# Two-layer conditional block on one core: another order of the first loads, and tile 5 copied ahead in step 0

## The chip, the cores and the metric

The kernel runs on one core of a Trainium2 chip. The metric is the device time of one execution in microseconds (us). The kernel before took 1658.18 us, the median of 3 runs (1657.36 to 1660.54). Its profile comes from one further execution, which took 1657.96 us; the profiled span of the core in it is 1656.2 us.

## What is computed

x is (64, 128, 512): 64 batches of 128 rows. Each batch b has a category (0 to 63) and an expert (0 to 15):

```python
# layer 0: one 512x512 matrix and bias per batch, chosen by category
x = x + (einsum('bsd,bdh->bsh', x, W[cat_ids]) + b[cat_ids][:, None, :])
# layer 1: fc1 to 2048, gelu, 384 shared columns, and 128 columns of the batch's expert
h = gelu(einsum('bnd,hd->bnh', x, fc1_w) + fc1_b, approximate=False)
shared = einsum('bnh,sh->bns', h, fc2_w) + fc2_b
expert = einsum('bnh,bph->bnp', h, experts_w[indices]) + experts_b[indices][:, None, :]
x = x + concatenate([shared, expert], axis=-1)
```

All of it is float32. The kernel makes each float32 product out of three matmuls on `fp32r` operands: each operand is split into a high half (a conversion on ScalarE) and a low half (the whole less the high half, on VectorE), and high x high, high x low and low x high are added up.

## The kernel before

The batches are worked through in 16 groups of four. A group's main work is 16 steps (`body`, c = 0 to 15). In step c TensorE does the fc1 of a block of 128 hidden columns (line 797: twelve matmuls of 512 columns into `ps_e` or `ps_h`), ScalarE its gelu (line 542), VectorE its two halves (`h_high`, line 671, and `h_low`), and TensorE, one step later, fc2 with the shared and the expert columns (line 812: twelve matmuls into `ps_out`). Experts' weights are transposed on VectorE (line 646) and halved. Layer 0 of the next group is spread over the steps of this one.

Nothing of that kind hides layer 0 of group 0: it is a stage of its own ahead of the steps, and the change is about it. It has 16 "slices", four for each of the four batches (`l0_slice`, line 772). A slice is a [128, 512] part of a category's matrix (256 KB), loaded by SyncE (`load_w`, line 340) into one of eight slots (four in `w_raw`, four in `e_blocks`), halved by ScalarE (`w_high`, line 491) and VectorE (`w_low`, line 610), and used in three matmuls (line 784). Slice j may be loaded once slice j - 8 is halved (`w_lo`), and ScalarE halves slice j three slices ahead of TensorE, and not before slice j - 5 is done (`l0_done`). The fourth slice of a batch comes with two matmuls that add the bias row (line 782, from `b0_rows`).

A batch's x is loaded as it is (`load_first_x`), transposed on TensorE (`turn_x`), and halved (`x_high`, `x_low`). When its four slices are done VectorE adds x to the product (`y_sum`, line 632), TensorE transposes the sum (`turn_y`, line 754) and it is halved into `y_t`, which fc1 reads; fc1 of group 0 wants all four batches.

Beside this the weights of fc1 and fc2 are prepared in 28 tiles (`PREP`): each is loaded by ScalarE's queue (`load_prep`, line 306), transposed on TensorE (`turn_prep`, line 761), and halved (`prep_high`, line 531, `prep_low`, line 604). Tiles 0 to 4 are done in the first stage (tile 0 at its start, tiles 1 to 4 ahead of slices 2, 5, 8 and 11), tiles 5 to 27 in the steps of group 0, two in each. From tile 5 on a transpose waits for the low half of the tile before it (`prep_lo`), since all go through the one bank `ps_t`. A tile's load waits until the tile before it in its buffer is transposed, and is issued behind that tile's `prep_high`.

The order of everything is written out by hand, one program for each engine, and each engine takes its instructions in that order; semaphores join them. SyncE's queue before the change issues `cats`, x of batch 0, waits for `cats`, and then goes slice by slice, with the bias row behind the first slice of a batch, the next batch's x behind the third, `exps` and `b1` behind slice 1, a wait for `exps` behind slice 2, and the reads of four expert indices from there (lines 399 to 418). ScalarE's queue issues tiles 0, 1 and 2 at its start. The experts' first quarter follows in SyncE's queue (lines 419 and 420).

Of the kernel before, what the change touches and what calls it, by code (L numbers as in the profile page):

```python
# [26 lines left out]
P = 128  # L27
# [3 lines left out]
def build(nc, x, cat_ids, exp_ids, l0_w, l0_b, fc1_w, fc1_b, fc2_w, fc2_b, exp_w, exp_b, out):  # L31
# [5 lines left out]
    GB = 4  # L37
# [9 lines left out]
    S0SLOTS = 5  # L47
    AHEAD = 3
    L0_STEPS = (2, 3, 5, 7, 9, 10, 11, 12)
    PSLOTS = 3  # L50
    Q = 32
    NPREP = NC + NS * NQ
# [2 lines left out]
    with ctx:  # L55
# [6 lines left out]
        def sem(name):  # L62
            return ctx.enter_context(nc.semaphore(name))
# [49 lines left out]
        cats_in = sem("cats_in")  # L113
        exps_in = sem("exps_in")
        prep_in = [sem(f"prep_in{i}") for i in range(PSLOTS)]
        w0_in = [sem(f"w0_in{i}") for i in range(W0SLOTS)]
        w_in = [sem(f"w_in{i}") for i in range(WSLOTS)]
        y_stored = sem("y_stored")
        y_blocks_in = sem("y_blocks_in")
# [41 lines left out]
        def after(eng, s, value):  # L161

            if not (isinstance(value, int) and value <= 0):
                eng.wait_ge(s, value)

        def first(G):

            return isinstance(G, int) and G == 0
# [102 lines left out]
        def w_slot(G, j):  # L271
            if first(G) and j % W0SLOTS >= WSLOTS + 2:
                return e_blocks[:, 1, j % W0SLOTS - WSLOTS - 2, :]
            return w_raw[:, j % (W0SLOTS if first(G) else WSLOTS), :]
# [39 lines left out]
        def _(sp):  # L314
# [8 lines left out]
            def load_first_x(b):  # L323

                sp.dma_start(resid[:, b, :], x[b, :, :]).then_inc(first_x_in[b], 16)

            def load_x_blocks(G, b):
# [7 lines left out]
                for i in range(P // Q):  # L335
                    src = x[bass.ds(G * GB + b, 1), :, :].rearrange("o (j q) (i n) -> i q (o j) n", q=Q, n=P)[i]
                    sp.dma_start(x_blocks[i * Q:(i + 1) * Q, :].rearrange("q (j n) -> q j n", n=P), src)\
                      .then_inc(x_blocks_in, 16)

            def load_w(G, j, cat):  # L340

                if first(G):
                    after(sp, w_lo, j - W0SLOTS + 1)
                else:
                    after(sp, w_lo, G * NC + j - WSLOTS + 1)
                k = j % KD
                src = l0_w[bass.ds(cat, 1), :, :].rearrange("o (p k) n -> k (o p) n", k=KD)[k]
                sp.dma_start(w_slot(G, j), src)\  # L348
                  .then_inc(w0_in[j % W0SLOTS] if first(G) else w_in[j % WSLOTS], 16)

            def load_b0(G, b, cat):
                after(sp, xb_ready, (G - 1) * GB + b)
# [2 lines left out]
            def category(G, b):  # L355
                return index(cats, G * GB + b, l0_w.shape[0])
# [40 lines left out]
                      .then_inc(out_stored, 16)  # L397

            sp.dma_start(cats[:, :], cat_ids.rearrange("(o n) -> o n", o=1)).then_inc(cats_in, 16)
            load_first_x(0)  # L400
            sp.wait_ge(cats_in, 16)
            first_experts = []
            for j in range(NC):
                if j % KD == 0:
                    cat = category(0, j // KD)
                load_w(0, j, cat)
                if j % KD == 0:
                    sp.dma_start(b0_rows[:, j // KD, :], l0_b[bass.ds(cat, 1), :]).then_inc(b0_rows_in[j // KD], 16)
                if j % KD == KD - 2 and j // KD + 1 < GB:
                    load_first_x(j // KD + 1)  # L410
                if j == 1:
                    sp.dma_start(exps[:, :], exp_ids.rearrange("(o n) -> o n", o=1)).then_inc(exps_in, 16)
                    sp.dma_start(b1[:, :].rearrange("p (u c) -> p u c", c=QUAD), fc1_b.rearrange("(u p c) -> p u c", p=P, c=QUAD))\
                      .then_inc(b1_in, 16)
                if j == 2:
                    sp.wait_ge(exps_in, 16)
                if 2 <= j < 2 + GB:
                    first_experts.append(index(exps, j - 2, exp_w.shape[0]))
            load_experts(0, 0, first_experts, range(GB))
            load_experts(0, 1, first_experts, [0])  # L420

# [67 lines left out]
        @block.scalar  # L489
        def _(act):  # L490
            def w_high(G, j):
                if first(G):
                    act.wait_ge(w0_in[j % W0SLOTS], 16 * (j // W0SLOTS + 1))
                else:
                    after(act, w_in[j % WSLOTS], 16 * ((G - 1) * (NC // WSLOTS) + j // WSLOTS + 1))
                after(act, l0_done, j - S0SLOTS + 1 if first(G) else G * NC + j - 1)
                nc.scalar.copy(split_slot(G, j)[:, 0, :], w_slot(G, j)).then_inc(w_hi, 1)  # L497

            def x_high(G, b):
                after(act, x_turned, G * GB + b + 1)  # L500

                after(act, l0_done, G * NC + (b - 1 if first(G) else b) * KD)
                nc.scalar.copy(x_halves(G, b)[:, 0, :, :], x_whole(G)).then_inc(x_hi, 1)  # L503

            def y_high(G, b):
                after(act, y_turned, G * GB + b + 1)
                after(act, fc1_done, G * NC)
                nc.scalar.copy(y_t[:, 0, :, b, :], y_whole(G, b)).then_inc(y_hi, 1)

            def store_y(G, b):  # L510
                after(act, y_ready, G * GB + b + 1)
                act.dma_start(y_rows[b, :, :], y[:, b, :]).then_inc(y_stored, 16)

            def load_y_blocks(G, b):
                after(act, y_stored, 16 * ((G - 1) * GB + b + 1))
                if b + 1 < GB:
                    after(act, x_turned, G * GB + b + 2)
                else:
                    after(act, y_turned, G * GB + b)
                for i in range(P // Q):  # L520
                    src = y_rows[b, :, :].rearrange("(j q) (i n) -> i q j n", q=Q, n=P)[i]
                    act.dma_start(x_blocks[i * Q:(i + 1) * Q, :].rearrange("q (j n) -> q j n", n=P), src)\
                       .then_inc(y_blocks_in, 16)

            def e_high(g, c):
                after(act, e_turned, g * NC + c + 1)
                after(act, fc2_done, (g * NC + c - 1) * GB)
                nc.scalar.copy(experts_of(c % 2, 0), e_whole[:, :].rearrange("p (q v n) -> p q v n", q=GB // 2, v=2))\  # L528
                    .then_inc(e_hi, 1)

            def prep_high(t):
                if t is None:
                    return
                act.wait_ge(prep_turned, t + 1)
                nc.scalar.copy(prep_dst(t, 0), four(prep_bank(t))).then_inc(prep_hi, 1)
                for u in prep_later(t):
                    load_prep(act, u)

            def gelu(g, c):
                after(act, fc1_done, g * NC + c + 1)  # L540
                after(act, h_lo, g * NC + c - 1)
                nc.scalar.activation(g_raw[:, c % 2, :], h_bank(c)[:, :], ACT.Gelu, bias=b1[:, c:c + 1])\  # L542
                    .then_inc(gelu_done, 1)

            for t in range(PSLOTS):
                load_prep(act, t)

            act.wait_ge(ident_ready, 1)
            nc.scalar.activation(g_raw[:, 0, 0:1], ident[:, 0:1], ACT.Gelu)
            prep_high(0)  # L550
            x_high(0, 0)
            for j in range(AHEAD):
                w_high(0, j)
            for j in range(NC):

                if j + AHEAD < NC:
                    w_high(0, j + AHEAD)
                if j % KD == 1 and j > KD:
                    y_high(0, j // KD - 1)
                if j % KD == KD - 2 and j // KD + 1 < GB:  # L560
                    x_high(0, j // KD + 1)
                for t in prep_beside(j):
                    prep_high(t)
            y_high(0, GB - 1)
            act.wait_ge(b1_in, 16)

            def body(g, more):
                for c in range(NC):

                    if more:  # L570
                        for j in slices_in(c):
                            w_high(g + 1, j)
                        for b in begun_in(c):
                            x_high(g + 1, b)
                    e_high(g, c)
                    if more:
                        for b in summed_in(c - 1):
                            store_y(g + 1, b)
                        for b in summed_in(c - 2):
                            load_y_blocks(g + 1, b)  # L580
                    gelu(g, c)
                    for n in range(PREP_RATE):
                        prep_high(prep_in_step(g, c, n))
                if more:
                    for b in range(GB):
                        y_high(g + 1, b)

            groups(act, body)


        @block.vector
        def _(dve):
# [112 lines left out]
            def body(g, more):  # L705
                for c in range(NC):
# [8 lines left out]
                    if c == 0 and not first(g):  # L715
                        for b in range(GB):
                            result(g - 1, b)
                    h_high(g, c)
                    prep_low(prep_in_step(g, c, 0))
                    h_low(g, c)  # L720
                    turn_next_e(g, c, more)
                    prep_low(prep_in_step(g, c, 1))
# [144 lines left out]
```

## Time and profile before

| | |
|---|---|
| median of 3 runs | 1658.18 us |
| the profiled execution | 1657.96 us |
| its span | 1656.2 us |
| TensorE matmuls busy | 1637.2 us (99%) |
| VectorE busy | 1314.8 us (79%) |
| ScalarE busy | 554.1 us (33%) |
| GpSimd busy | 214.4 us (13%) |
| DMA | 243.44 MB, mean 147 GB/s |

A page has one row for each engine (PE is TensorE's matmuls, PEld its weight loads, DVE VectorE, ACT ScalarE, POOL GpSimd, SP SyncE; a q behind the name is that engine's instruction queue). Its chain is the work that ended last, followed back from the end: each piece to what released it, or to the instruction before it on its engine. "issue" in it is time in which an engine waited for nothing that the profile shows. Times inside a trace count from the start of the span. A line number can be that of a helper: all low halves, for one, are written by line 602.

### The profile page before, as it was taken

The numbers are of one execution on the slowest core, as the hardware profiler recorded it, in microseconds if no ns is written. First come the engines' busy times: TensorE is split into PE (matmuls) and PEld (weight loads), VectorE is DVE, ScalarE is ACT, GpSimd is POOL, SyncE is SP. The second block draws the span as 40 slices with busy tenths as digits, with TensorE's granted clock in tenths as the row PEclk, the third lists the DMA queues.
The fourth block names the chain that finished last, engine by engine and source line by source line (L and its number), as shares of the span: only waits on it lengthen the run. The fifth ranks groups of instructions, "written<-read, shape, count | busy, mean of one in ns | idle before, by whom it ended". The sixth has DMA issues, their size and how long they took to land.

```text
span 1656.2 us, 27997 instructions
## 1 busy us (share of the span) xinstructions
PE 1637.2 (99%) x7064; PEld 1320.6 (80%) x7064; DVE 1314.8 (79%) x2004; ACT 554.1 (33%) x926; POOL 214.4 (13%) x195
## 2 busy tenths in 40 slices
PE   7999999999999999999999999999999999999999
PEld 4788887888888888888888888888888887888887
DVE  5787978788787887877878788787878878788865
ACT  4343333333333333333333333333333333333321
POOL 0110200202020120200202011020200202002100
PEclk8899999999999999999999999999999999999999
DMA  7665555546465454664546555454654546555410
GB/s 218 175 187 136 164 151 155 144 139 167 130 175 145 143 157 115 174 161 142 153 115 183 146 161 142 141 159 133 168 157 135 152 114 180 162 144 148 134 52 26
DMA packets 303178, 243.44 MB, mean 147 GB/s; under 512 B 34152, under 2 KB 234984, under 8 KB 303084
## 3 DMA queue, kind: packets, MB, share of 16 engines
q1 hardware_dynamic: 255852, 203.75, 45.1%
q10 hardware_dynamic: 47232, 38.82, 7.7%
q14 instruction: 82, 0.67, 0.1%
q8 instruction: 12, 0.20, 0.1%
HBM read 209.93 MB, written 32.51 MB: 146 GB/s over the span
## 4 chain that ended last, share of the span: by engine, by line
PE 97%; issue 1%; SPq 1%; DMA 1%; DVE 1%; ACT 0%; DVEq 0%
PE ps_out L812 42%; PE ps_e L797 21%; PE ps_h L797 21%; PE ps_y L784 10%; PE ps_t L745 1%; PE ps_h L784 0%; SPq L316 0%; DMA x_blocks<-in_x 0%; DMA e_blocks<-in_L_cond_W 0%; DMA exps<-in_itok_B 0%; SPq L348 0%; PE ps_e L745 0%; PE ps_h L782 0%; DVE w_split L602 0%; DVE y L637 0%
## 5 line engine op out<-in xcount | busy, mean ns | idle before, releaser
L812 PE MATMUL ps_out<-w2e,h 128*128 128x512 f32 x3072 | 756.6, 395 | 0.0
L812 PEld LDWEIGHTS ps_out<-w2e,h 128*128 128x128 f32 x3072 | 575.5, 188 | 137.8
L797 PE MATMUL ps_e<-y_t,w 128*128 128x512 f32 x1536 | 378.2, 396 | 0.5 <-DVE y_t L602 0.5
L797 PE MATMUL ps_h<-y_t,w 128*128 128x512 f32 x1536 | 376.4, 394 | 0.0
L797 PEld LDWEIGHTS ps_e<-y_t,w 128*128 128x128 f32 x1536 | 289.1, 189 | 68.9 <-issue 3.8
L797 PEld LDWEIGHTS ps_h<-y_t,w 128*128 128x128 f32 x1536 | 289.6, 189 | 65.3
L646 DVE STREAM_TRANSPOSE e_whole<-e_blocks 128x512 f32<-128x512 f32 x256 | 279.1, 1090 | 0.0
L528 ACT CAST w2e<-e_whole 128x512 fp32r<-128x512 f32 x256 | 158.7, 620 | 355.3 <-DVE e_whole L646 355.3
L671 DVE CAST h<-g_raw 128x512 fp32r<-128x512 f32 x256 | 125.6, 491 | 182.8 <-ACT g_raw L542 182.7
L461 POOL TENSOR_TENSOR x_raw<-x_raw,b_all 128x512 f32<-128x512 f32 x60 | 87.3, 1455 | 1286.3 <-DMA x_raw<-in_x 1238.5
L497 ACT CAST w_split<-w_raw 128x512 fp32r<-128x512 f32 x244 | 145.2, 619 | 213.3 <-DMA w_raw<-in_L_cond_W 122.5
L602 DVE TENSOR_TENSOR w2e<-e_whole,w2e 128x512 fp32r<-128x512 f32 x256 | 199.8, 780 | 18.1 <-ACT w2e L528 17.9
L602 DVE TENSOR_TENSOR w_split<-w_raw,w_split 128x512 fp32r<-128x512 f32 x244 | 164.6, 708 | 43.1 <-ACT w_split L497 42.9
L784 PE MATMUL ps_y<-w_split,x_t 128*128 128x512 f32 x732 | 190.8, 396 | 3.2 <-DVE w_split L602 2.7
L602 DVE TENSOR_TENSOR h<-g_raw,h 128x512 fp32r<-128x512 f32 x256 | 186.3, 728 | 8.4
L542 ACT ACTIVATE g_raw<-ps_e,b 128x512 f32<-128x512 f32 x128 | 88.1, 689 | 247.5 <-PE ps_e L797 241.5
L784 PEld LDWEIGHTS ps_y<-w_split,x_t 128*128 128x128 f32 x732 | 137.2, 189 | 37.4 <-issue 5.1
L542 ACT ACTIVATE g_raw<-ps_h,b 128x512 f32<-128x512 f32 x128 | 88.0, 688 | 167.3 <-PE ps_h L797 159.6
L664 DVE CAST w2e<-w2e 128x512 fp32r<-128x512 f32 x256 | 116.4, 455 | 0.0
L471 POOL TENSOR_TENSOR resid<-y,b_all 128x384 f32<-128x384 f32 x64 | 87.1, 1361 | 75.5 <-DMA out<-resid 74.5
L617 DVE STREAM_TRANSPOSE x_whole_t<-x_blocks 128x512 f32<-128x512 f32 x60 | 64.8, 1079 | 37.9 <-DMA x_blocks<-in_x 37.9
L503 ACT CAST x_t<-x_whole_t 128x512 fp32r<-128x512 f32 x60 | 37.2, 620 | 60.0 <-DVE x_whole_t L617 60.0
(68 smaller groups left out, 459.3 us busy)
## 6 DMA issues: line engine op xcount, KB each, us to landing
e_blocks<-in_L_cond_experts_w SPq DMA_DIRECT2D x1024, 64.0 KB, 2.5
w_raw<-in_L_cond_W SPq DMA_DIRECT2D x248, 256.0 KB, 4.0
out<-resid SPq DMA_DIRECT2D x64, 256.0 KB, 2.6
b_all<-in_L_cond_b SPq DMA_DIRECT2D x60, 256.0 KB, 4.2
x_raw<-in_x SPq DMA_DIRECT2D x60, 256.0 KB, 4.7
x_blocks<-in_x SPq DMA_DIRECT2D x240, 64.0 KB, 3.2
y_rows<-y ACTq DMA_DIRECT2D x60, 256.0 KB, 3.5
x_blocks<-y_rows ACTq DMA_DIRECT2D x240, 64.0 KB, 2.7
```

Source lines behind the costliest of these rows:

```text
L461: nc.gpsimd.tensor_tensor(x_raw[:, :], x_raw[:, :], b0_all[:, :], ALU.add).then_inc(xb_ready, 1)
L471: nc.gpsimd.tensor_tensor(resid[:, b, 0:SHARED], y[:, b, 0:SHARED], b2_all[:, :], ALU.add)
L497: nc.scalar.copy(split_slot(G, j)[:, 0, :], w_slot(G, j)).then_inc(w_hi, 1)
L528: nc.scalar.copy(experts_of(c % 2, 0), e_whole[:, :].rearrange("p (q v n) -> p q v n", q=GB // 2, v=2))\
L542: nc.scalar.activation(g_raw[:, c % 2, :], h_bank(c)[:, :], ACT.Gelu, bias=b1[:, c:c + 1])\
L602: return nc.vector.tensor_tensor(dst, whole, high.bitcast(F32), ALU.subtract)
L646: nc.vector.transpose(e_whole[:, :].rearrange("p (a q) -> p a q", q=Q), src).then_inc(e_turned, 1)
L664: nc.vector.tensor_copy(ring[:, c % 2, :, :, 1, :], w2[:, :, c, SHARED - P:].unsqueeze(2).to_broadcast([P, 2, GB // 2, P]))\
L671: nc.vector.tensor_copy(h[:, c % 2, 0, :], g_raw[:, c % 2, :]).then_inc(h_hi, 1)
L784: last = nc.tensor.matmul(l0_bank(G, b)[:, :], x_halves(G, b)[:, a, k, :], split_slot(G, j)[:, w, :], start=(k == 0 and n == 0), stop=(k = ...
L797: last = nc.tensor.matmul(h_bank(c)[:, :], w1[:, w, k, c * P:(c + 1) * P], y_t[:, a, k, :, :].rearrange("p b s -> p (b s)"), start=(k == 0 ...
L812: last = nc.tensor.matmul(ps_out[b][:, :], h[:, c % 2, a, b * S:(b + 1) * S], fc2_columns(c, c % 2, w, b), start=(c == 0 and n == 0), stop ...
```

## The change

SyncE issues `cats` and `exps`, waits for `cats` only, and then issues the slices by the list `FIRST_W`: slices 0 to 3 each by itself, the others in pairs of neighbours, one transfer of 512 KB for a pair. The bias row and the next batch's x go behind the last slice of a batch. The wait for `exps` and the four index reads go behind all slices. x of batch 0 and `b1` move to ScalarE's queue; tiles 1, 2 and 3 are loaded from there behind the conversions of slices 0, 1 and 4. In step 0 of group 0, ScalarE's copy of tile 5 stands ahead of the gelu and VectorE's low half ahead of `h_high`.

```diff
+    FIRST_W = ((0,), (1,), (2,), (3,), (4, 5), (6, 7), (8, 9), (10, 11), (12, 13), (14, 15))
-        w0_in = [sem(f"w0_in{i}") for i in range(W0SLOTS)]
+        w0_in = [sem(f"w0_in{i}") for i in range(len(FIRST_W))]
+            def load_first_w(n, cat):
+                j, m = FIRST_W[n][0], len(FIRST_W[n])
+                after(sp, w_lo, j + m - W0SLOTS)
+                k, slot = j % KD, j % W0SLOTS
+                dst = w_raw[:, slot:slot + m, :] if slot < WSLOTS + 2 else e_blocks[:, 1, slot - WSLOTS - 2:slot - WSLOTS - 2 + m, :]
+                src = l0_w[bass.ds(cat, 1), :, :].rearrange("o (p k) n -> (o p) (k n)", k=KD)[:, k * D:(k + m) * D]
+                sp.dma_start(dst.rearrange("p k n -> p (k n)"), src).then_inc(w0_in[n], 16)
             sp.dma_start(cats[:, :], cat_ids.rearrange("(o n) -> o n", o=1)).then_inc(cats_in, 16)
-            load_first_x(0)
+            sp.dma_start(exps[:, :], exp_ids.rearrange("(o n) -> o n", o=1)).then_inc(exps_in, 16)
             sp.wait_ge(cats_in, 16)
-            first_experts = []
-            for j in range(NC):
-                if j % KD == 0:
-                    cat = category(0, j // KD)
-                load_w(0, j, cat)
-                if j % KD == 0:
-                    sp.dma_start(b0_rows[:, j // KD, :], l0_b[bass.ds(cat, 1), :]).then_inc(b0_rows_in[j // KD], 16)
-                if j % KD == KD - 2 and j // KD + 1 < GB:
-                    load_first_x(j // KD + 1)
-                if j == 1:
-                    sp.dma_start(exps[:, :], exp_ids.rearrange("(o n) -> o n", o=1)).then_inc(exps_in, 16)
-                    sp.dma_start(b1[:, :].rearrange("p (u c) -> p u c", c=QUAD), fc1_b.rearrange("(u p c) -> p u c", p=P, c=QUAD))\
-                      .then_inc(b1_in, 16)
-                if j == 2:
-                    sp.wait_ge(exps_in, 16)
-                if 2 <= j < 2 + GB:
-                    first_experts.append(index(exps, j - 2, exp_w.shape[0]))
+            for n, slices in enumerate(FIRST_W):
+                b = slices[0] // KD
+                if slices[0] % KD == 0:
+                    cat = category(0, b)
+                load_first_w(n, cat)
+                if slices[-1] % KD == KD - 1:
+                    sp.dma_start(b0_rows[:, b, :], l0_b[bass.ds(cat, 1), :]).then_inc(b0_rows_in[b], 16)
+                    if b + 1 < GB:
+                        load_first_x(b + 1)
+            sp.wait_ge(exps_in, 16)
+            first_experts = [index(exps, b, exp_w.shape[0]) for b in range(GB)]
             load_experts(0, 0, first_experts, range(GB))
...
-                for u in prep_later(t):
-                    load_prep(act, u)
+                if t > 0:
+                    for u in prep_later(t):
+                        load_prep(act, u)
...
-            for t in range(PSLOTS):
-                load_prep(act, t)
+            act.dma_start(resid[:, 0, :], x[0, :, :]).then_inc(first_x_in[0], 16)
+            load_prep(act, 0)
+            act.dma_start(b1[:, :].rearrange("p (u c) -> p u c", c=QUAD), fc1_b.rearrange("(u p c) -> p u c", p=P, c=QUAD))\
+               .then_inc(b1_in, 16)
...
             for j in range(AHEAD):
                 w_high(0, j)
+                if j + 1 < PSLOTS:
+                    load_prep(act, j + 1)
             for j in range(NC):
                 if j + AHEAD < NC:
                     w_high(0, j + AHEAD)
+                if j == 1:
+                    load_prep(act, PSLOTS)
...
+                    if c == 0:
+                        prep_high(prep_in_step(g, c, 0))
                     gelu(g, c)
-                    for n in range(PREP_RATE):
+                    for n in range(1 if c == 0 else 0, PREP_RATE):
                         prep_high(prep_in_step(g, c, n))
...
+                    if c == 0:
+                        prep_low(prep_in_step(g, c, 0))
                     h_high(g, c)
-                    prep_low(prep_in_step(g, c, 0))
+                    if c > 0:
+                        prep_low(prep_in_step(g, c, 0))
```

## Rows read from the trace of the kernel before

**Rows 1.** The page: each engine's busy us, share of the span, instructions.

```profile
PE 1637.2 (99%) x7064; PEld 1320.6 (80%) x7064; DVE 1314.8 (79%) x2004; ACT 554.1 (33%) x926; POOL 214.4 (13%) x195
```

**Rows 2.** Waits of TensorE, whole span: total us, times, longest us.

```profile
PE ps_t L745 <- issue: 3.4, 2, 2.0
PE ps_y L784 <- DVE w_split L602: 2.7, 1, 2.7
PE ps_h L784 <- DVE h L602: 2.0, 1, 2.0
```

**Rows 3.** The chain in order of time, 0 to 90: start us, us, what.

```profile
0.72 1.23 DMA cats<-in_itok_B
...
4.32 3.47 DMA exps<-in_itok_B
...
12.16 4.09 DMA e_blocks<-in_L_cond_W
...
17.61 0.60 DVE h L602
...
22.05 1.28 PE ps_h L784 x3
23.33 0.85 PE ps_t L745 x4
...
28.79 0.47 PE ps_e L745 x4
29.25 0.70 PE ps_y L784 x3
...
31.60 1.05 PE ps_y L782 x2
32.65 0.91 PE ps_y L784 x3
...
38.46 0.70 DVE y L637
...
46.80 2.02 issue
```

**Rows 4.** Busy us by engine in stretches of time, then clock, DMA share, GB/s.

```profile
0.00:12.20 12.20, 4.85 (x14) 3.42 (x14) 2.76 (x5) 4.51 (x7) 0.84 (x7) 1.00 0.74 225
12.20:19.00 6.80, 4.67 (x19) 2.71 (x19) 4.11 (x7) 3.96 (x7) 0.00 (x0) 1.00 0.71 229
19.00:25.80 6.80, 6.05 (x21) 4.59 (x20) 5.25 (x9) 3.66 (x7) 0.00 (x0) 0.50 0.99 345
25.80:39.50 13.70, 12.83 (x55) 8.31 (x55) 8.50 (x14) 5.38 (x10) 0.00 (x0) 1.00 0.63 139
39.50:46.30 6.80, 6.25 (x19) 4.89 (x19) 2.70 (x4) 1.20 (x2) 0.00 (x0) 0.50 0.87 234
...
49.70:53.10 3.40, 3.40 (x10) 2.62 (x9) 2.17 (x4) 1.09 (x2) 2.37 (x3) 0.50 0.44 147
```

**Rows 5.** DMA issues at 2.92 and 4.65: KB each, us from issue to landing.

```profile
w_raw<-in_L_cond_W SPq DMA_DIRECT2D x1, 256.0 KB, 4.6
...
b<-in_L_cond_fc_b SPq DMA_DIRECT2D x1, 8.0 KB, 4.3
```

**Rows 6.** Instructions in order of time: start us, us, engine, line, what [idle before].

```profile
8.98 2.90 PE L784 MATMUL ps_y<-w_split,x_t 128*128 128x512 f32 x6 [2.73 <-DVE w_split L602]
...
12.88 0.62 ACT L497 CAST w2e<-w_raw 128x512 fp32r<-128x512 f32 x1 [0.76 <-DMA w_raw<-in_L_cond_W]
...
16.31 0.89 SPq L348 DMA_DIRECT2D w_raw<-in_L_cond_W  x2
...
22.06 14.79 SPq L383 DMA_DIRECT2D e_blocks<-in_L_cond_experts_w  x20
...
41.63 5.17 PE L797 MATMUL ps_e<-y_t,w 128*128 128x512 f32 x12 [0.55 <-DVE y_t L602]
...
48.03 0.69 DVE L602 TENSOR_TENSOR w<-ps_t,w 128x512 fp32r<-128x512 f32 x1
```

More of the change, by code:

```diff
@@ L338, in load_x_blocks @@
                       .then_inc(x_blocks_in, 16)
-            def load_w(G, j, cat):
[L342 to L349, printed above, removed]
+            def load_first_w(n, cat):
[5 more added lines that the diff above has]
+                sp.dma_start(dst.rearrange("p k n -> p (k n)"), src).then_inc(w0_in[n], 16)
+            def load_w(G, j, cat):
+                after(sp, w_lo, G * NC + j - WSLOTS + 1)
+                src = l0_w[bass.ds(cat, 1), :, :].rearrange("o (p k) n -> k (o p) n", k=KD)[j % KD]
+                sp.dma_start(w_slot(G, j), src).then_inc(w_in[j % WSLOTS], 16)
             def load_b0(G, b, cat):
@@ L492, in w_high @@
                 if first(G):
-                    act.wait_ge(w0_in[j % W0SLOTS], 16 * (j // W0SLOTS + 1))
+                    act.wait_ge(w0_in[[j in slices for slices in FIRST_W].index(True)], 16)
                 else:
```

## The prediction

> **What bounds the kernel now.** I read the page first: TensorE is busy for 1637.2 us, 99% of the span [rows 1]. So only time in which TensorE stands still, or runs at its low clock, can be won, and what is won early is kept: nothing behind it waits for anything but TensorE. Then TensorE's own waits: the long ones are a transpose in line 745 (3.4 us in two pieces, released by nothing that the profile shows) and two in line 784, for the converted weights and x of the first stage (2.7 and 2.0 us) [rows 2]. All but 1.4 us of them lie before 50 us. Third, the chain in order of time through those 50 us [rows 3]. It stands on SyncE at first: the load of `exps`, 3.47 us, holds back slice 3 and all behind it; then slice 5, issued at 12.16, takes 4.09 us to land; then VectorE's queue at 0.60 us an operation; from 20.07 on TensorE itself. fc1 of group 0 begins at 41.63 [rows 6]. After its first step comes 2.02 us of nothing [rows 3]: tile 6's transpose is behind a wait on `prep_lo` for tile 5, and VectorE makes that low half only at 48.03 [rows 6], since tile 5's copy stands behind the gelu on ScalarE and behind `h_high` on VectorE. Last, the stretches between changes of the clock [rows 4]: 1.00 from 12.2 to 19, 0.50 to 25.8, 1.00 to 39.5, 0.50 to 46.3, and 0.50 once more from 49.7 to 53.1. The column also says 1.00 before 12.2, but six matmuls there took 2.90 us [rows 6], the 1.28 us for three of a low stretch and not the 0.70 of a high one [rows 3]: the start runs at 1.2 GHz too.
>
> **SyncE's issues.** Before, slice 0 goes out at 2.92 [rows 6] and slice 5 only at 12.16 [rows 3]. Removed from between them: x of batch 0, `exps` with its wait, `b1`, and the reads of the expert indices. `cats` still goes first and must land, so slice 0 stays at 2.92. Two slices back to back cost 0.89 us [rows 6], 0.45 each: slices 1, 2, 3 at 3.4, 3.8, 4.3, b0's row at 4.8, x of batch 1 at 5.3, a category read of about 0.9 (estimate, from the 0.89 of two issues), the pair 4-5 at 6.6, 6-7 at 7.1, row and x of batch 2 by 8.1, pair 8-9 at 9.4, 10-11 at 9.9. The later pairs wait for `w_lo` 6 and 8.
>
> **What they land as.** Slice 0 took 4.6 us from issue to landing [rows 5]. With x of batch 0 and tile 0 alone ahead of it, and two tiles of fc1's weights no longer in its way, I put slice 0 at 6.5 (it was 2.92 + 4.6 = 7.5), and the next three 0.7 apart: 256 KB at the 345 GB/s that stretch 19 to 25.8 shows [rows 4] is 0.76. So slice 3 lands by 8.8; issued at 4.3 instead of after the `exps` wait. x of batch 1 comes by 9.6, tile 1 (now issued only when slice 0 has landed) by 10 to 12, pair 4-5 by 11 to 12.5, pair 6-7 by 13 to 15. `b1` is now ahead of slice 0: 8 KB took 4.3 us [rows 5], as long as a slice, and in it the engines may lose up to a slice's 0.8 us; I take half.
> A rule of the Trainium skill speaks against this step: "DMA: Bandwidth & Descriptors", section Specifications, has pieces below 512 bytes make the engine read, modify and write, and `b1` is made of 16-byte pieces. Its section "Issuing engines are not separate DMA queues" adds that ScalarE's queue gives no bandwidth of its own. By the two, slice 0 would gain nothing (7.5) and the sum below would be 1 us smaller; the 4.3 us for 8 KB agree with the first.
>
> **TensorE's first stage.** x of batch 0 is not ready earlier (tile 0 and x issue as early as before, at 0.7 and 1.2), so slice 0 starts at 8.3 instead of 8.98. At the low clock slices 0 and 1 (1.28 each), x 1 and tile 1 (0.85 each) bring it to 12.5; slice 2 and slice 3 with its bias (0.70, 1.05 and 0.91 at the high clock) to 15.3. The start of slice 4 was 18.27. Slice 4's halves are made by 13 to 15, hidden. From there on everything is on TensorE: slices 4 to 15 are nine at 0.70 and three at 1.05 + 0.91, and between them stand eight transposes at 0.47 (y 0 to 2, x 2 and 3, tiles 2 to 4) [rows 3]: 6.3 + 5.9 + 3.8 = 16.0, so 31.3. VectorE has some 26 operations of 0.60 in that time, 15.6 us, and ScalarE as many of 0.62 [rows 3, 6]: they fit, barely, so the order in which they wait can cost a gap of 1 us at y of batch 0 (`y_sum(0)` stands behind slice 6's low half, pair 6-7 by 15). The end of the stage (sum, transpose, two halves) took from 38.46, where y's last sum starts [rows 3], to 41.63, 3.2 us, and I keep 3.0: fc1 at 34.3, which is 7.3 us earlier. Of these, 3.4 are the low stretch from 19.0 to 25.8 [rows 4], 6.8 us at half speed, that goes because the 2.0 us of idleness ahead of it goes.
> The other end of this term: the transfers bind. 25 tiles of 256 KB (16 slices, 4 x, 5 prepared) are 6.55 MB; at the 225 GB/s of the first 12.2 us [rows 4] that is 29 us, counted from 2.0, where `cats` as the first transfer landed [rows 3]: the last slice at 31.1, and behind it 0.6 + 0.7 of halves, 2.0 of slice and bias, 3.0 of end and some 0.6 between them: 38.0, a gain of 3.6. At 345 GB/s it would be 21.0, with room. Nearest is the second, since SyncE issues back to back, as it did from 19 on; I take 6.5 of 7.3.
>
> **Step 0.** Tile 5 is copied ahead of gelu and `h_high`, beside fc1's twelve matmuls (5.17 us [rows 6]): its transpose is done before fc1, and e_high (0.62), its own halves (0.62, 0.69) follow the transpose of the experts: ready some 3 us after fc1's start. The 2.02 us go. What is late next is tile 7's transpose, which wants tile 6's low half; VectorE now has h_low and a 1.1 us transpose of the experts ahead of that, and fc1(1) at the high clock is only 2.8 us long: 0.4 comes back. Term: 1.6 us (between 0 and 2.0). If the cover by fc1 fell away, gelu would be pushed back by the 0.6 of the copy; gelu waits for all twelve matmuls, so it isn't. The low stretch from 49.7 to 53.1 begins behind this idleness and costs half of its 3.4, 1.7 us [rows 4]; between 0 and 1.7 I take 1.0. The one from 39.5 to 46.3 begins behind the end of the stage, which stays: kept, 3.4 us.
>
> **Moved, at no cost.** Nothing of group 1 goes out earlier than its buffers come free, the experts (20 issues in 14.8 us [rows 6]) start at some 19 instead of 22.06 and are wanted at 34, tile 3's load at 11 instead of 5.4 is wanted at 21. If this cover failed, tile 3 would cost its delay. The 1.4 us that line 745's wait has beside the 2.0 [rows 2] lies at 86 us, in a later step: it stays, or moves by as much.
>
> **Sum.** 6.5 + 1.6 + 1.0 = 9.1 us from the profiled execution's 1657.96 (span 1656.2 and 1.8 around it) is 1648.9; the median shown, 1658.18, stands 0.2 higher: 1649.
>
> **Rivals.** (a) The transfers bind, as worked out: 3.6 + 1.6 and up to 1.0 for the clock, 5.2 to 6.2: 1652.5. For it: the first 12.2 us had their DMA engines at 0.74 for 225 GB/s [rows 4]. Against: that stretch holds the wait for `exps`. (b) The clock falls once more inside the first stage: one stretch of 6.8 us at half speed costs 3.4: 1652.5. For it: so it did at 19.0. Against: 25.8 to 39.5, the same mixture of work without long gaps, stayed high [rows 4]. (c) The other side: the clock, low at the start, does not rise at 12.2 and stays low through the dense stretch. Its 18.8 us (12.5 to 31.3) at the high clock would be 37.6 at the low one; 18.8 lost against 11 gained leaves 8 slower: 1666. It decides from about 21 us of low clock on, where half of that eats 10.5. For it: transposes and one-row bias matmuls are much of the work. Against: each low stretch past 12.2 was over within 6.8 us [rows 4].
> The Trainium skill's "TensorE: Matmul & The Clock Gate", section "Part 4: PE-mode transpose", says that transposes don't count as activity for the clock, which speaks for (b) and (c): there is a transpose group between most slices. By it the sum would be 1652.5 or 1666; the stretch at 0.50 from 19 to 25.8, which begins behind idleness but lasts through 6 us of busy TensorE, agrees in part. (d) The step-0 gap stays, because tile 7 or the experts take its place: 2 to 3 smaller, 1651.5. (e) All goes well and the stretch of 39.5 goes too: 1643.5.
>
> **Chances.** Forecast 0.50, (a) 0.14, (b) 0.13, (c) 0.03, (d) 0.10, (e) 0.06, and 0.04 for something that I don't see and that leaves no gain. A measurement tells about 0.2%, 3.3 us, from no change. Faster: 0.88, within 0.2%: 0.08, slower 0.04. The range takes in (a), (b), (d), (e): 1643.5 to 1655; the forecast's own is 1646 to 1652.
>
> **What would show it.** Slices 1 to 3 issued by 4.3 and landed by 9; slice 4 on TensorE near 15.3, y of batch 0 near 16; no idleness of TensorE over 1 us between 15 and 31; fc1 of group 0 at 34.3 to 35; no idle time between it and tile 6's transpose; a single low stretch behind 12.2. It is wrong if pair 4-5 or tile 1 lands after 13, if VectorE's operations stand back to back while TensorE waits, or if 0.50 comes up before 30 us.

## The result and the profile after

The changed kernel took 1675.05 us (median of 4 executions, 1674.58 to 1676.2) where the kernel before took 1658.09 (its profiled execution counted in): ratio 1.0114, 95% interval 1.0097 to 1.0131. (The ratios here and below are those on record with their intervals; the quotient of the two medians can differ, here 1.0102.) It is 17 us slower by the medians; 9 us faster had been forecast. The profiled execution took 1674.58 us, its span is 1672.8.

TensorE's waits over the whole span, in us, times and the longest; they answer to [rows 2]:

```profile
PE ps_y L795 <- DVE x_t L610: 20.0, 13, 2.6
PE ps_out L756 <- DMA prep_raw<-in_L_cond_fc_w: 5.5, 2, 4.6
PE ps_y L795 <- DVE w_split L610: 2.1, 1, 2.1
PE ps_t L756 <- issue: 1.6, 2, 1.3
```

The 2.02 us of step 0 are gone, as forecast. But the first row did not exist before: 20.0 us in 13 waits for `x_t`, one in each pass of the loop over the groups. From 100 us on, the kernel before had this and nothing else:

```profile
PE ps_y L784 <- DVE x_t L602: 0.3, 1, 0.3
```

So the first stage did what it was meant to, and the loss lies where nothing was changed. TensorE's instructions in the first stage, in order of time (start, us; idle before in brackets), beside [rows 6]:

```profile
8.60 2.90 PE L795 MATMUL ps_y<-w_split,x_t 128*128 128x512 f32 x6 [2.09 <-DVE w_split L610]
11.29 1.06 PE L756 MATMUL ps_t<-ident,resid 128*128 128x128 f32 x4
13.30 0.75 PE L756 MATMUL ps_out<-ident,prep_raw 128*128 128x128 f32 x4 [0.95 <-DMA prep_raw<-in_L_cond_fc_w]
...
16.54 0.86 PE L795 MATMUL ps_h<-w2e,h 128*128 128x512 f32 x3
17.96 0.75 PE L756 MATMUL ps_e<-ident,y 128*128 128x128 f32 x4 [0.56 <-DVE y L645]
...
36.74 4.57 PE L808 MATMUL ps_e<-y_t,w 128*128 128x512 f32 x12 [0.92 <-DVE y_t L610]
```

fc1 of group 0 starts at 36.74 for 41.63 [rows 6], and group 1's first fc1 at 151.2 for 160.1: 8.9 us won by then, against a forecast of 9.1. Group 1 then takes 100.5 us and each of the 13 groups behind it 101.0 to 104.6, where the kernel before takes 100.13 to 100.74; from group 1's start to group 15's it is 1428.8 for 1403.3 us. Of these 25.5 us, 20.0 are the waits above; 3.4 are two low stretches of the clock, 6.8 us at half speed together, each of which begins within 1 us of the end of such a wait (of 2.15 and 2.62 us). A group without and one with such a stretch:

```profile
150.00:251.00 101.00, 100.93 (x436) 81.36 (x435) 84.06 (x126) 33.48 (x56) 14.18 (x12) 1.00 0.54 149
251.00:356.00 105.00, 102.85 (x437) 82.66 (x436) 83.73 (x127) 33.76 (x56) 13.67 (x12) 0.98 0.49 143
```

(Stretches of time: busy us of TensorE, its loads, VectorE, ScalarE, GpSimd; clock, DMA share, GB/s.) Some 2 us stay unexplained.

Where the 13 waits come from stands in the chain, here from 1065 to 1085 (start, us, what):

```profile
1066.45 0.05 SPq L301
1066.50 3.22 issue
1069.72 0.06 SPq L301
1069.78 0.06 issue
1069.84 0.28 SPq L317
1070.12 0.05 issue
1070.17 0.16 SPq L317
1070.33 1.45 issue
```

Line 301 is the loop itself. SyncE branches back, stands 3.22 us, does three instructions of the loop, and stands 1.45 us again, waiting for no semaphore. The kernel before has the first pause (2.55 to 4.02 us in its 13 passes) and not the second; the changed kernel has both in all 13, the second of 1.44 to 1.74 us. SyncE's DMAs around the same loop end, first before, then after:

```profile
455.27 1.92 SPq L390 DMA_DIRECT2D be_all<-in_L_cond_experts_b  x4
464.66 0.86 SPq L348 DMA_DIRECT2D w_raw<-in_L_cond_W  x2
465.70 0.33 SPq L353 DMA_DIRECT2D b_all<-in_L_cond_b  x1
466.22 0.33 SPq L320 DMA_DIRECT2D x_raw<-in_x  x1
466.65 1.89 SPq L337 DMA_DIRECT2D x_blocks<-in_x  x4
```

```profile
452.14 1.91 SPq L395 DMA_DIRECT2D be_all<-in_L_cond_experts_b  x4
462.77 0.86 SPq L354 DMA_DIRECT2D w_raw<-in_L_cond_W  x2
463.81 0.33 SPq L358 DMA_DIRECT2D b_all<-in_L_cond_b  x1
464.32 0.33 SPq L321 DMA_DIRECT2D x_raw<-in_x  x1
464.76 1.89 SPq L338 DMA_DIRECT2D x_blocks<-in_x  x4
```

From the last `be_all` to `x_blocks` it is 9.46 us before and 10.71 after. `x_blocks` is what VectorE turns into the next group's x, which TensorE wants in step 2. The kernel before had almost no room there: in the one pass with a first pause of 4.02 us it waited too, the 0.3 us above. Queue 14, whose packets are of the kind "instruction" and so carry code, shows the same (queue, kind: packets, MB, share), before and after:

```profile
q14 instruction: 82, 0.67, 0.1%
```

```profile
q14 instruction: 95, 0.78, 0.2%
```

13 packets more, one for each pass. Each is of 8 KB. In one pass, from one branch back to the next, there are five before and six after:

```profile
q14 instruction: 5, 0.04, 0.1%
```

```profile
q14 instruction: 6, 0.05, 0.2%
```

Set beside SyncE's instructions, they come at fixed places of the loop. Before: one in the pause at the branch back and one right behind it, then as SyncE has done 115, 247 and 371 instructions. After: one in each of the two pauses, one behind the second, then at some 143, 270 and 392. So one packet goes with about 128 instructions, and one is asked for ahead of the code that runs.

### The profile page after: what moved, and what is told of

It reads as the page before. It is cut to its first block, busy times and chain, and to the rows that moved or that the text cites. A ratio compares the mean times of both kernels' runs of the same rounds, so it can differ in the third digit from the quotient of the medians.

```text
span 1672.8 us, 27979 instructions
## 1 busy us (share of the span) xinstructions
PE 1637.8 (98%) x7064; PEld 1319.1 (79%) x7064; DVE 1317.4 (79%) x2004; ACT 555.8 (33%) x926; POOL 213.5 (13%) x195
## 4 chain that ended last, share of the span: by engine, by line
PE 78%; issue 8%; SPq 7%; DMA 4%; DVE 3%; ACT 1%; DVEq 0%
PE ps_out L823 32%; PE ps_h L808 17%; PE ps_e L808 17%; PE ps_y L795 10%; DMA x_blocks<-in_x 3%; SPq L317 2%; SPq L395 1%; SPq L388 1%; SPq L338 1%; DVE e_whole L654 1%; PE ps_t L756 1%; DVE w_split L610 1%; SPq L354 1%; ACT g_raw L542 1%; DVE x_t L610 1%
## 5 line engine op out<-in xcount | busy, mean ns | idle before, releaser
L610 DVE TENSOR_TENSOR w2e<-e_whole,w2e 128x512 fp32r<-128x512 f32 x256 | 200.3, 783 | 18.1 <-ACT w2e L527 18.0
L610 DVE TENSOR_TENSOR w_split<-w_raw,w_split 128x512 fp32r<-128x512 f32 x244 | 170.9, 733 | 38.2 <-ACT w_split L496 38.0
L795 PEld LDWEIGHTS ps_y<-w_split,x_t 128*128 128x128 f32 x732 | 137.1, 190 | 60.0 <-DVE w_split L610 25.5
L470 POOL TENSOR_TENSOR resid<-y,b_all 128x384 f32<-128x384 f32 x64 | 82.8, 1294 | 75.3 <-DMA out<-resid 75.3
```

The source lines that it names most:

```text
L470: nc.gpsimd.tensor_tensor(resid[:, b, 0:SHARED], y[:, b, 0:SHARED], b2_all[:, :], ALU.add)
L610: return nc.vector.tensor_tensor(dst, whole, high.bitcast(F32), ALU.subtract)
L795: last = nc.tensor.matmul(l0_bank(G, b)[:, :], x_halves(G, b)[:, a, k, :], split_slot(G, j)[:, w, :], start=(k == 0 and n == 0), stop=(k = ...
```

## The experiments

Theory L (layout): the loop's head lies 20 instructions earlier in SyncE's code than before (the loop begins behind 460 of SyncE's instructions in the trace, before behind 480; its own length is 406 in both), 3 instructions ahead of a point at which more code must be fetched. The 20 are eight loads (six by the pairing, two moved to ScalarE) and twelve register instructions. Rival P (phase): the shorter first stage puts the engines in another phase, and the groups settle into a slower pattern. Rival D: the pairs, or the moved loads, disturb the transfers. The kernel before has a median of 1656.4 us on the chip of the first four runs, 1654.6 on that of the next four, 1655.5 on that of the last four; each run is compared with its own chip's.

**after_nop4** and **before_nop236**, **before_nop240**

```diff
+            for _ in range(4):
+                sp.nop()
             load_experts(0, 0, first_experts, range(GB))
```

That is the edit of the first; the other two have 236 (15 in each of steps 0 to 11 of group 0, 14 in the others) and 240 (15 in each) in the kernel before.

> The changed kernel with four instructions that do nothing on SyncE, ahead of the experts' first loads of the first stage; nothing else differs. Theory L (layout of the code): in the changed kernel SyncE's loop begins 3 instructions ahead of a boundary of its instruction fetch, so each of the 13 passes waits for the code twice (2.5 to 4.1 us at the loop's head, 1.43 to 1.74 us behind its third instruction), x_blocks of the next group land that much later, and TensorE waits 20.0 us in 13 times. Four instructions more put the head on the far side: the second wait goes, DVE x_t waits fall from 20.0 to under 1 us, three low stretches of the clock past 100 us fall to none, and the time is 1649 to 1653. Theory P (phase): the earlier first stage leaves the engines in another phase to one another, and the later groups settle into a slower pattern; four instructions, some 0.3 us of SyncE's time, change nothing: 1675. Theory D (the 512 KB pairs or the moved x and b1 disturb the transfers for good): 1675 too.

> The kernel before with 236 instructions that do nothing on SyncE, 15 in each of steps 0 to 11 of group 0 and 14 in each of steps 12 to 15, spread so that none delays a load by more than about 1 us. Theory L with blocks of 256 instructions: SyncE's loop head, 20 instructions later in the kernel before than in the changed one, comes again 3 instructions ahead of a boundary (20 less 256 is -236): 13 second waits of 1.4 to 1.7 us, TensorE waits some 20 us for x_t, and the kernel before gets as slow as 1675 to 1680 with its first stage untouched. Theory L with another block size that does not divide 256: no second wait there. Theories P and D: 1658, at most 1 to 2 more for the instructions themselves.

> As before_nop236 with 15 in each of the 16 steps, 240 in all, four more. Theory L: the head is 1 past the boundary, no second wait for code, 1658 to 1660. If the 236 instructions themselves cost time, this one costs the same: both slow. The difference between the two is the layout's alone: 17 to 21 us by theory L, none by P and D.

These three tell nothing of the layout. The empty instructions are not in the traces: SyncE has 865 instructions ahead of its first branch back with and without the four, 885 with and without the 236 or 240, and the second pause stands behind the third instruction of the loop as before them. They are repetitions: the changed kernel again at 1674.46 (1.0115 of before, 1.0081 to 1.0149), the kernel before at 1656.91 and 1656.51 (1.0009 and 1.0002). They have a use as such: the start of group 0's fc1, 41.63 in [rows 6], was 39.22 and 39.65 in these two, and 40.34 for the changed kernel's 36.74. Between executions of what is the same program by its trace, the first stage ends up to 2.4 and 3.6 us apart.

**step0_only**: the kernel before with the two edits of step 0.

```diff
+                    if c == 0:
+                        prep_high(prep_in_step(g, c, 0))
                     gelu(g, c)
-                    for n in range(PREP_RATE):
+                    for n in range(1 if c == 0 else 0, PREP_RATE):
                         prep_high(prep_in_step(g, c, n))
...
+                    if c == 0:
+                        prep_low(prep_in_step(g, c, 0))
                     h_high(g, c)
-                    prep_low(prep_in_step(g, c, 0))
+                    if c > 0:
+                        prep_low(prep_in_step(g, c, 0))
```

> The kernel before with only the step-0 part of the change (ScalarE's copy of tile 5 ahead of the gelu, VectorE's low half ahead of h_high). SyncE's code is that of before. By the prediction: the 2.02 us at 46.8 go, and the low stretch of the clock at 49.7 with them (1.7 more): 1654.5 to 1656. Theory L: no second wait for code, SyncE as before, the same 1654.5 to 1656. Theory P: any shift of the phase by 2 us could bring the slower pattern: up to 1670.

1654.05 for 1656.4: 0.9983 (0.9973 to 0.9994), 2.4 us (1.0 to 4.5 by the interval), close to the 2.6 that the prediction has for this part (1.6 and 1.0). A shift of 2 us brings no slower pattern.

**after_read2**: real instructions in place of the empty ones.

```diff
+            for _ in range(2):
+                index(exps, 0, exp_w.shape[0])
             load_experts(0, 0, first_experts, range(GB))
```

> The four empty instructions of after_nop4 were not in the program that ran: SyncE's stream had the same 865 instructions ahead of its first branch back. Here the changed kernel reads two expert indices more than it uses, ahead of the experts' first loads: three real instructions each, 1.3 us of SyncE's time where it has room. Theory L: the loop's head moves from 3 instructions ahead of the boundary to 3 behind it; the second wait for code goes in all 13 passes, the x_t waits of TensorE fall from 20.0 us to under 2, 13 instruction packets fewer on queue 14 (82 for 95): 1647 to 1652. Theory P: 1675.

1654.11 us: 0.9993 of before (0.9982 to 1.0003). Six instructions, 871 for 865 ahead of the branch, take away the 17 us: no pass has the second pause. Queue 14 has 82 packets again, and the waits of TensorE are:

```profile
PE ps_out L758 <- DMA prep_raw<-in_L_cond_fc_w: 5.6, 2, 4.5
PE ps_t L758 <- issue: 2.4, 2, 1.3
PE ps_y L797 <- DVE w_split L612: 2.1, 1, 2.1
PE ps_y L797 <- DVE x_t L612: 1.3, 3, 0.5
```

P and D fall: stage, pairs and moved loads are all there. But it is above the 1647 to 1652 expected; see after_read2_tile1.

**before_inc236** and **before_inc240**: the reverse, the slowness brought into the kernel before. Semaphore increments stay in the code where empty instructions don't: 1121 and 1125 instructions ahead of the branch for 885. The edit with 236; the other has 15 in each step, and both declare the unused semaphore `pad_done`.

```diff
+                    if first(g):
+                        for _ in range(15 if c < 12 else 14):
+                            sp.sem_inc(pad_done, 1)
                     if c == 0 and not first(g):
                         store(g - 1)
```

> The kernel before with 236 increments of an unused semaphore on SyncE, spread over the steps of group 0 (15 in steps 0 to 11, 14 in 12 to 15), in place of the empty instructions that fell away. Theory L with blocks of 256 instructions: the loop's head, 17 behind a boundary in the kernel before, comes to 3 ahead of the next: 13 second waits, 13 instruction packets more, 1673 to 1680. Another size of block, or theory P: 1656 to 1660.

> As before_inc236, with four increments more (15 in each step): theory L puts the head 1 behind the boundary: no second wait, 1656 to 1661, 17 us under before_inc236. If the increments themselves cost the time, both are slow alike.

1678.86 (two executions; 1.0144, 1.0121 to 1.0167) against 1657.74 (eight; 1.0015, 1.0003 to 1.0027): four instructions apart, 21 us. With 236, all 13 passes have a second pause of 1.43 to 1.73 us behind the third instruction; with 240 none has. Queue 14 has 97 packets in the one and 84 in the other. Waits for `x_t`, first 236, then 240:

```profile
PE ps_y L788 <- DVE x_t L606: 18.7, 13, 2.9
```

```profile
PE ps_y L788 <- DVE x_t L606: 1.6, 2, 1.3
```

The places that hurt are thus 256 instructions apart (20 earlier, or 236 later). The Trainium skill, "Runtime: NRT & Kernel Launch", section "Instruction fetch mechanics", says that code comes in blocks of 256 instructions, one fetched while the one before runs, and that a taken branch to code outside of the two blocks at hand must wait for its fetch. The traces agree with the manner: some 3 us of pause at each branch back of the 406-instruction loop, and a second pause where the next stretch of code begins before there was time to fetch it. They don't agree with the size: the 8 KB packets come at every 128 instructions or so, five or six in a pass. These runs show a repeat at 256, which is also twice 128; a head 128 instructions away was not tried, and by the packets it would hurt as well. Nor was it tried how far ahead of such a point a head still hurts. An estimate: from the end of the first pause to the end of the second it is some 2 us, so a head with less than 2 us of instructions ahead of the point would pay a part.

**after_later**: is it `x_blocks` alone that carries the damage?

```diff
-                idx = first_experts if first(g) else [index(exps, g * GB + b, exp_w.shape[0]) for b in range(GB)]
+                idx = first_experts
                 for c in range(NC):
                     if more:
                         load_l0_in(g + 1, c)
+                    if c == 0 and not first(g):
+                        idx = [index(exps, g * GB + b, exp_w.shape[0]) for b in range(GB)]
```

> The changed kernel with the four reads of expert indices at the head of SyncE's loop moved behind the loads of step 0, x_blocks among them (4 x 0.64 = 2.6 us earlier); the same instructions in another order, so the head stays 3 ahead of the boundary. Theory L: both waits for code stay (2.5 to 4.1 and 1.4 to 1.7 us in each pass), but x_blocks go out 1.0 us earlier than in the kernel before, and TensorE waits for none of it: 1647 to 1651. It says that the damage is the lateness of x_blocks and nothing else of the second wait. Theory P: a slower pattern that is no matter of x_blocks stays: 1665 to 1675.

1656.13: 1.0015 (1.0005 to 1.0026). Both pauses are still in each pass (13 second ones, 1.42 to 1.69 us), no wait for `x_t` is left, and the time is 1.5 us above the kernel before where the changed kernel's repetition was 18.1 above it, so the way through `x_blocks` is right. But the groups take 100.1 to 101.7 us, 5.1 over 14 times 100.14, so 1647 to 1651 was too good: something behind `x_blocks` is late too. TensorE has 1.4 us more in waits for `w_split` (3.5 us in 5 times, for 2.1 in one); the rest isn't traced further.

**after_later_read2**: both.

> The changed kernel with both: the two extra index reads (three instructions each, so SyncE's loop head is behind the boundary) and the four reads at the loop's head moved behind step 0's loads. after_read2 had one wait for code in each pass and still 1.3 us of x_t waits in 3 times; after_later had both waits for code, no x_t wait, but groups of 100.1 to 101.7 us instead of 100.14. Theory L+S (layout, and little slack in SyncE's queue at the head of a group): neither is left, groups take 100.14 to 100.3: 2 to 5 us under after_read2, 1649 to 1652 where the kernel before is 1654.6. Rival: moving the reads only moves the lateness to the experts' loads, and the time is that of after_later, 1656.

1651.6: 0.9978 (0.9968 to 0.9988), 3.9 us under the kernel before. The groups from 2 on take 100.14 to 100.19 us. The rival, that the lateness only moves to the experts' loads and the time is after_later's, falls. With a layout that has no second pause the reads' place still seems worth some 2.5 us (0.9978 for after_read2's 0.9993; the two intervals just overlap; groups 1 to 14 take 1402.6 us for 1405.0). That it is so because the first pause varies (2.5 to 4.1 us) is argued and not shown.

**after_read2_tile1** and **after_all**

```diff
             load_prep(act, 0)
+            load_prep(act, 1)
             act.dma_start(b1[:, :].rearrange("p (u c) -> p u c", c=QUAD), fc1_b.rearrange("(u p c) -> p u c", p=P, c=QUAD))\
...
-                if j + 1 < PSLOTS:
+                if 0 < j < PSLOTS - 1:
```

> after_read2 with tile 1 of fc1's weights loaded at the start of ScalarE's queue, behind tile 0 and ahead of b1, instead of behind slice 0's conversion. In the four traces of the changed stage tile 1 landed at 13.3 to 14.6, and TensorE stood 0.95 to 1.84 us before its transpose, with the low clock from 16.0 in two of them. Theory T (tile 1 is the stage's new stall): it lands by 7, the wait goes, slice 2 starts near 12.2 instead of 14.2, fc1 of group 0 at 36 to 38 instead of 39.4 to 40.3, 1.5 to 3 us under after_read2. Rival: with 256 KB more ahead of slice 0, slices 0 to 3 land 0.7 later each and TensorE waits for them instead: no gain.

> All three together: the reads behind step 0's loads, the two extra reads, and tile 1 at the start. If the effects are separate, the best of all: 1647 to 1650 where the kernel before is 1654.6. If the first stage's gain is eaten by the clock (a low stretch elsewhere), 1650 to 1653.

1651.75 (0.9984, 0.9973 to 0.9996) and 1648.46 (0.9963, 0.9949 to 0.9977). fc1 of group 0 starts at 35.63 and 36.59. For tile 1 alone that is some 1.5 us by the ratios (0.9984 for after_read2's 0.9993), with intervals that overlap: the stage ends earlier, but the gain in the whole is not clear of noise; in this trace TensorE waits 1.36 us at 43.55 for the load of a later tile. TensorE's first instructions in after_all, with no wait for tile 1 between x 1 and slice 2:

```profile
9.30 2.90 PE L800 MATMUL ps_y<-w_split,x_t 128*128 128x512 f32 x6 [2.09 <-DVE w_split L615]
11.99 1.05 PE L761 MATMUL ps_t<-ident,resid 128*128 128x128 f32 x4
12.84 1.06 PE L761 MATMUL ps_out<-ident,prep_raw 128*128 128x128 f32 x4
13.55 1.52 PE L800 MATMUL ps_y<-w2e,x_t 128*128 128x512 f32 x3
```

Slices 0 and 1 start 4.05 us after tile 0's transpose, as in the changed kernel (8.60 and 4.55); tile 0 itself comes at 5.11 and 5.25 in these two, where it came at 4.49 to 5.18 with tile 1 later. after_all is 7.05 us under the kernel before by the medians, some 6 by the ratio (3.8 to 8.4), and has the lowest median of all.

**stage_only**: after_read2 with step 0 as it was before.

> after_read2 without the step-0 part: the first stage's part of the change by itself, with a sound layout. The step-0 part by itself gave 2.35 us (step0_only). By the prediction the stage is worth 6.5 us: 1648 to 1650. By after_read2, which as a whole gave only 0.5 us, it is worth nothing or less: 1654.6 to 1657, the kernel before or slower.

1655.12: 1.0002 (0.9991 to 1.0013). No gain of the first stage's part can be seen as it stands. Its trace shows why:

```profile
13.80 0.75 PE L753 MATMUL ps_out<-ident,prep_raw 128*128 128x128 f32 x4 [1.44 <-DMA prep_raw<-in_L_cond_fc_w]
14.30 0.94 PE L792 MATMUL ps_y<-w2e,x_t 128*128 128x512 f32 x3
15.18 1.53 PE L790 MATMUL ps_y<-y,g_raw 1*128 1x512 f32 x2
16.64 1.65 PE L792 MATMUL ps_y<-w2e,x_t 128*128 128x512 f32 x3
```

Slice 2's three matmuls take 0.94 us and slice 3's 1.65, at the low clock that comes up at 15.8 and lasts to 22.6, behind 1.44 us of waiting for tile 1. Of six traces with this stage (tile 1 late), three have this low stretch (16 to 23 us), two have their matmuls at the pace of the low clock up to some 21 us, and only the one first shown had neither: fc1 at 36.74 in that, 39.4 to 40.3 in the five others, where the stage of before has 39.2 to 41.6 in six traces. The means are 39.3 and 40.1.

## Why the prediction was wrong

- **The step that failed** is "Moved, at no cost", with its "Nothing of group 1 goes out earlier than its buffers come free", and the premise that what is won early is kept, since nothing behind it waits for anything but TensorE. It treated SyncE's code as without a length. Twenty instructions fewer moved the loop's head to 3 ahead of a fetch of code; the second pause in each pass made `x_blocks` late, and that cost 20.0 us of waits and 3.4 of clock. Shown from both sides, by after_read2 and by before_inc236 against before_inc240. No rival of mine had it: the one on the slower side, (c), was the clock in the first stage, and no low stretch of that stage lasted past 23.1. Its ground, transposes and one-row matmuls in the mixture, holds at most in part: two of six traces stayed low up to 21 us, but in the profiled execution the same mixture ran at 1.00 from 23.0 to 36.7.
- The premise had a hint against it: line 784's 0.3 us wait for `x_t` in the groups, which showed that room to be near zero.
- **Step 0** was right in mechanism: the 2.02 us went, and 0.36 came back at tile 7's transpose in the profiled execution (forecast 0.4). In size, the part measured 2.4 us alone for 2.6, with an interval too wide (1.0 to 4.5) to test the two terms apart.
- **SyncE's issues** came as worked out up to 9.33: slices 1 to 3 by 4.56, pairs at 6.69 and 7.20; the pair 10-11 went out at 11.26 for 9.9. Slice 0's start was near too (8.60 for 8.3). `b1` landed 3.3 us after its issue and slice 0 at 6.3 (3.4 after its issue, 4.3 in the slowest of the six traces), so the loss counted for small pieces, which the prediction took from the Trainium skill's "DMA: Bandwidth & Descriptors", section Specifications, did not show at this size.
- **The first stage's 6.5 us** was mis-sized. Tile 1 was put at 10 to 12 and landed at 13.3 to 14.6, 6.7 to 7.3 us after its issue in the full queues. I had named its limit, 13, but not that the clock falls, in three of six traces, behind the idleness that follows. And [rows 4] are of an execution slower in the stage (41.63) than five others with the same stage (39.2 to 40.4): its three low stretches, which cost 8.5 us (1.7 to 5.2 in those five), were partly chance, and I counted 4.4 of them as gain. Something like rival (b) is what usually happened. With tile 1 early the stage ends at 35.6 to 36.6, near the 35.1 that the sum has.
- **The 8.9 us by group 1** agree with the sum's 9.1 by luck. The stage gave 4.9 for 6.5, and group 0's steps 4.0 for 2.6: 1.7 of gap, and some 2.3 of clock. Both traces lie at the end of their spread as well: group 1 began at 160.1 where four other traces of that code, with instructions added on SyncE alone, have 154.5 to 158.0, and at 151.2 where the changed kernel's repetition has 153.8.

## What to carry over

Code ahead of a loop is part of the loop's cost where an engine's code is fetched anew in each pass: compare the pause at the branch back, the gaps in the first instructions behind it, and the packets of the queue that carries code, whenever the number of instructions ahead changes, and put loads that someone waits for before register work at a loop's head. A wait of 0.3 us in one pass of thirteen is a warning that the others have no room. And a first stage whose clock falls in a different place in each execution isn't measured by one profile.

## What the runs showed of the hardware

- SyncE's branch back in a loop of 406 or 407 instructions costs 2.5 to 4.2 us in every trace; VectorE's and ScalarE's loop ends (221 and 170 instructions), 0.26 to 0.28 and 0.15 to 0.16 us. A further fetch, 3 instructions behind the head, costs 1.42 to 1.74 us more.
- SyncE's code came in packets of 8 KB, one for about 128 instructions: five a pass without the second pause, six with it.
- Two positions of the loop's head 256 instructions apart both hurt; the change from hurting to harmless lies within 4. A position 128 away was not tried.
- Behind a pause of TensorE in a loop that is otherwise dense, the clock sometimes fell for 3.4 us: in 2, 3 and 3 of 13 passes of the three kernels with the second pause and its waits, each time behind a pause of 2.0 to 2.9 us; pauses of 2.2 and 2.6 us in the same traces had no such stretch behind them.
